# Two expert-choice layers of an eight-layer network: five stages become one, and the expert products move between the search steps

## The reference, cut to what matters

```python
logits = xf @ router_w + router_b          # 2048 x 16
S = softmax(logits, axis=-1)
G, idx = top_k(S.T, k)                     # k = 2048 / 16 = 128, per expert
out = einsum('ekh,hd->ekd', xf[idx], expert_w) + expert_b
y[idx] += G[..., None] * out
```

## Time and profile before

| what | before |
|---|---|
| median of 3 runs | 3193.43 us |
| the profiled execution, its time | 3191.56 us |
| its span, first to last instruction | 3188.7 us |
| PE busy | 89% |
| DVE busy | 53% |
| ACT busy | 26% |
| POOL busy | 31% |
| mean granted TensorE clock | 0.929 of full speed |
| first expert-choice layer, DVE's first to last instruction | 2483.52 to 2594.17 us |
| second one | 3070.68 to 3180.31 us |

### The profile page before, as it was taken

The page is one execution under the profiler, slowest core; times in us unless marked ns, Lnnn a source line. Parts: engine busy times, 40 slices in busy tenths (PEclk is TensorE's granted clock), DMA queues, the critical chain, the costliest instruction groups (busy, mean ns, idle before and its releaser), DMA issues. The chain is left out here.

```text
span 3188.7 us, 46399 instructions
## 1 busy us (share of the span) xinstructions
PE 2822.7 (89%) x15610; PEld 1928.5 (60%) x15610; DVE 1675.7 (53%) x4583; ACT 827.0 (26%) x1344; POOL 974.7 (31%) x1089
## 2 busy tenths in 40 slices
PE   7999999998999999999979999999999538888872
PEld 3444458885556555788757777777777423443451
DVE  5566646666564655466644333333335556555555
ACT  2333344442101011444422222222221002222210
POOL 0000036775444444667721222222221001212200
PEclk8999999999999999999989999999998757887885
DMA  3000020000000000100000000000000000000000
GB/s 137 1 0 0 0 99 1 0 0 1 1 0 0 0 0 0 80 0 0 0 14 14 14 1 14 14 14 1 14 1 1 23 0 1 1 0 0 0 0 26
DMA packets 6281, 37.88 MB, mean 12 GB/s; under 512 B 272, under 2 KB 4368, under 8 KB 4496
## 3 DMA queue, kind: packets, MB, share of 16 engines
q1 hardware_dynamic: 6160, 36.34, 2.9%
HBM read 34.24 MB, written 2.10 MB: 11 GB/s over the span
## 5 line engine op out<-in xcount | busy, mean ns | idle before, releaser
L590 PE MATMUL banks<-back 32*128 32x512 f32 (+3 forms) x1088 | 366.3, 603 | 30.0 <-DVE back L600 20.7
L365 PE MATMUL banks<-moe_parts 128*128 128x512 f32 x1536 | 369.9, 397 | 13.8 <-POOL moe_parts L445 8.9
L817 ACT ACTIVATE back<-banks 128x1024 f32<-128x1024 f32 (+3 forms) x256 | 217.1, 863 | 460.9 <-PE banks L711 460.6
L365 PEld LDWEIGHTS banks<-moe_parts 128*128 128x128 f32 x1536 | 289.1, 192 | 77.2 <-issue 18.9
L1433 PE MATMUL banks<-lin_parts 128*128 128x512 f32 x1152 | 305.9, 411 | 19.3 <-DVE lin_parts L1684 15.5
L1619 DVE TENSOR_TENSOR ffn_pack<-banks,back 128x512 f32<-128x512 f32 x128 | 88.4, 691 | 351.0 <-PE banks L1446 350.9
L711 PE MATMUL banks<-back 32*128 32x512 f32 (+3 forms) x1024 | 242.2, 585 | 20.6 <-DVE back L833 12.5
L1433 PEld LDWEIGHTS banks<-lin_parts 128*128 128x128 f32 x1152 | 212.5, 193 | 67.2 <-issue 21.0
L590 PEld LDWEIGHTS banks<-back 32*128 32x128 f32 x1088 | 135.8, 200 | 185.7 <-DVE back L604 77.7
L1749 POOL TENSOR_TENSOR ffn_pack<-ffn_pack 128x256 f32<-128x256 f32 x112 | 82.9, 741 | 497.2 <-ACT ffn_pack L1582 497.2
L604 DVE TENSOR_REDUCE back<-banks 128x1 f32<-128x512 f32 x272 | 176.3, 686 | 80.2 <-PE banks L590 75.5
(11 more groups left out here) (224 smaller groups left out, 5235.7 us busy)
## 6 DMA issues: line engine op xcount, KB each, us to landing
back<-p_raw SPq DMA_DIRECT2D x8, 1024.0 KB, 4.8
back<-p SPq DMA_DIRECT2D x1, 7696.0 KB, 21.2
ffn_pack<-ffn SPq DMA_DIRECT2D x1, 6144.0 KB, 26.7
back<-p SPq DMA_DIRECT2D x1, 5152.0 KB, 15.0
back<-p SPq DMA_DIRECT2D x2, 1792.0 KB, 8.0
out<-x SPq DMA_DIRECT2D x1, 2048.0 KB, 7.5
x<-x_in SPq DMA_DIRECT2D x1, 1536.0 KB, 12.7
small_pack<-small SPq DMA_DIRECT2D x1, 619.0 KB, 4.9
```

The lines of the kernel that those rows point to most:

```text
L365: mm = nc.tensor.matmul(bank[:], up[:, n % 2, a, which, kd, :], xp[:, b, kd, :], start=((a, b, kd) == (0, 0, 0)), stop=((a, b, kd) == (1, ...
L590: nc.tensor.matmul(bank[:, 0:n], qs[head_rows[j], hg, qi * P:(qi + 1) * P], ks[head_rows[j], hg, 0:n], start=True, stop=True).then_inc(D.f ...
L817: nc.scalar.activation(pt[:, (kt % 2) * 2 + pair, :, q0:T], two[:, :, q0:T], ACT.Exp, scale=0.25).then_inc(A.free.s, 2)
```

## The change

The five blocks become one, without loops.

- Statistics are taken for batches 1 to 3 only (12 tiles). The four instances of the transposed tokens have memory of their own: `c.xt` for batch 0, `xts` for the others. ACT copies each transposed batch out of a pair of PSUM banks in one instruction, where DVE copied two halves.
- The router products are separated from the expert products. PE does all the router products first. The 16 expert products (one for each tile of 128 tokens) follow: two before the transpose of the probabilities, and one behind each of the first 14 counts of the search.
- ACT takes the expert products out of PSUM, two tiles at a time, and POOL adds the bias.
- The search is 15 steps written out. `thr` is updated and `bit` shifted (into a second copy) while PE sums the counts, and one instruction builds the next candidates from `bit`, `thr` and the digit.
- DVE fills `ones`, `thr` and `bit` at the start of the layer; ACT runs one exponential there. A transpose that nothing used and its copy are gone.

```diff
-    D.open(KD + 2 + 2)
     ...
-            with pe.Fori(0, B) as it:
     ...
-                turn_xn(nc, c, pe, it)
+    REST = (B - 1) * NT
     ...
+    xt_of = [c.xt] + [xts[:, b] for b in range(B - 1)]
+    xn_of = [None, c.xn, xn2, c.xn]
+
+    def after_count(u):
+
+        return range(0, 2) if u < 0 else range(u + 2, u + 3) if u + 2 < B * NT else ()
+
     with nc.Block() as block:
         @block.tensor
     ...
+            def turn(b):
+                pe.wait_ge(c.xn_ready.s, c.xn_ready.at(0, b))
+                pe.wait_ge(S.free.s, S.may_fill(0))
+                pair = S.fill("xt", b)
     ...
+            def router(b):
+                if b:
+                    pe.wait_ge(S.free.s, S.released(0, "xt", b))
+                pe.wait_ge(D.free.s, D.may_fill(0))
     ...
+            def product(n):
+                b, i = n // NT, n % NT
+                if i % 2 == 0:
+                    pe.wait_ge(O.free.s, O.may_fill(0))
     ...
+            router(0)
+            for b in range(1, B):
+                turn(b)
+                router(b)
+            for n in after_count(-1):
+                product(n)
+            pe.wait_ge(c.s_ready.s, c.s_ready.at(0, 1))
     ...
+            for u in range(STEPS):
+                pe.wait_ge(c.sum_ready.s, c.sum_ready.at(0, u + 1))
+                pe.wait_ge(D.free.s, D.may_fill(0))
+                bank = D.fill("count", u)
+                nc.tensor.matmul(bank[:, 0:3], same, cnt[:], start=True, stop=True).then_inc(D.full.s, 1)
+                for n in after_count(u):
+                    product(n)
     ...
         @block.scalar
         def _(act):
+            act.wait_ge(c.s_small.s, 16)
+            nc.scalar.activation(warm, c.ident[:, 0:1], ACT.Exp)
+            for b in range(1, B):
+                act.wait_ge(S.full.s, S.may_read(0))
+                pair = S.read("xt", b)
+                nc.scalar.activation(xts[:, b - 1], pair[:], ACT.Identity).then_inc(S.free.s, 1)
     ...
+            for n in range(B * NT // 2):
+                keep_y(n)
 
         @block.vector
     ...
+            moments(nc, c, c.ve, lambda n: c.x[:, 1 + n // NT, n % NT, :], REST)
+            inverse_sqrt(nc, c, c.ve, c.mv[:, 0:REST, 1])
+            norm(1)
+            norm(2)
+            keep_logits(0)
+            dve.wait_ge(S.full.s, S.full.at(0, 1))
+            norm(3)
+            for b in range(1, B):
+                keep_logits(b)
     ...
-            with dve.Fori(0, ROUNDS) as it:
-                c.ve.turn(dve, it)
-                link = c.ve.link
-                for u in range(STEPS):
-
-                    link(nc.vector.tensor_tensor(cand[:], thr.to_broadcast([P, 3]), bit[:], ALU.bitwise_or))
     ...
-                    link(nc.vector.tensor_tensor(add[:], digit[:], bit[:, 0:1], ALU.mult))
-                    nc.vector.tensor_scalar(bit[:], bit[:], 2, None, ALU.logical_shift_right)
-                    link(nc.vector.tensor_tensor(thr[:], thr[:], add[:], ALU.bitwise_or))
     ...
+            for u in range(STEPS):
+                now, later = bit[:, u % 2], bit[:, (u + 1) % 2]
     ...
+                ins.then_inc(c.sum_ready.s, 1)
+                if u:
+                    nc.vector.tensor_tensor(thr[:], thr[:], add[:], ALU.bitwise_or)
+                nc.vector.tensor_scalar(later, now, 2, None, ALU.logical_shift_right)
     ...
+                link(nc.vector.tensor_tensor(add[:], digit[:], now[:, 0:1], ALU.mult))
+                if u + 1 < STEPS:
+                    link(nc.vector.scalar_tensor_tensor(out=cand[:], in0=later, scalar=add[:],
+                                                        in1=thr.to_broadcast([P, 3]), op0=ALU.bitwise_or,
+                                                        op1=ALU.bitwise_or))
     ...
+            dve.wait_ge(c.y_ready.s, c.y_ready.at(0, B * NT // 2))
     ...
+        @block.gpsimd
+        def _(pool):
+            pool.wait_ge(c.s_small.s, 16)
+            for n in range(B * NT // 2):
+                b, h = n // 2, n % 2
+                pool.wait_ge(O.free.s, O.released(0, "y", b, h))
+                ys = y[:, b, 2 * h:2 * h + 2, :]
+                nc.gpsimd.tensor_tensor(ys, ys, eb.unsqueeze(1).to_broadcast([P, 2, DM]), ALU.add)\
+                    .then_inc(c.y_ready.s, 1)
```

More of the change, by code:

```diff
@@ L1865, in _ @@
[L1865 to L1872, removed]
-                for i in range(NT):
[L1874 to L1881, removed]
-                                            bank[:, 0:2 * E6].rearrange("p (a e) -> p a e", a=2),
-                                            rb.unsqueeze(1).to_broadcast([P, 2, E6]), ALU.add)\
-                        .then_inc(D.free.s, 1)
-                for h in range(2):
-                    dve.wait_ge(D.full.s, D.may_read(it))
-                    bank = D.read("out", h)
-                    nc.vector.tensor_tensor(y[:, it, 2 * h:2 * h + 2, :],
-                                            bank[:].rearrange("p (a d) -> p a d", a=2),
-                                            eb.unsqueeze(1).to_broadcast([P, 2, DM]), ALU.add)\
-                        .then_inc(D.free.s, 1)
-                keep_xt(nc, c, dve, it)
@@ L1894, in _ @@
[L1894 to L1904, removed]
-    c.ex_ready.open(1)
-    c.ve.open(4)
-    tiles = lg[:].rearrange("p b i e -> p (b i) e")
-    with nc.Block() as block:
+            def turn(b):
+                pe.wait_ge(c.xn_ready.s, c.xn_ready.at(0, b))
+                pe.wait_ge(S.free.s, S.may_fill(0))
+                pair = S.fill("xt", b)
+                for kd in range(KD):
+                    for i in range(NT):
+                        mm = nc.tensor.transpose(pair[:, kd, i * P:(i + 1) * P],
+                                                 xn_of[b][:, i, kd * P:(kd + 1) * P], c.ident[:])
+                mm.then_inc(S.full.s, 1)
@@ new lines, in _ @@
+            pe.wait_ge(c.sum_ready.s, c.sum_ready.at(0, STEPS + 2))
+            pe.wait_ge(D.free.s, D.may_fill(0))
+            bank = D.fill("taken")
+            nc.tensor.matmul(bank[:, 0:1], same, cnt[:, 0:1], start=True, stop=False)
+            nc.tensor.matmul(bank[:, 0:1], earlier, cum[:, SEG_T - 1:SEG_T], start=False, stop=True)\
+                .then_inc(D.full.s, 1)
+            pe.wait_ge(c.sum_ready.s, c.sum_ready.at(0, STEPS + 3))
+            pe.wait_ge(D.free.s, D.may_fill(0))
@@ L1952, in _ @@
             nc.vector.tensor_copy(ss[:], bank[:, 0:SEG_T]).then_inc(D.free.s, 1)
-            dve.wait_ge(D.full.s, D.may_read(0))
-            bank = D.read("unused")
-            nc.vector.tensor_copy(cnt[:], bank[:, 0:3]).then_inc(D.free.s, 1)
-            nc.vector.memset(ones[:], 1.0)
-            nc.vector.memset(thr[:], 0)
-            for k in range(3):
-                nc.vector.memset(bit[:, k:k + 1], (k + 1) << (BITS - 2))
-    D.close(1)
-    O.take(c.banks[7:8])
-    O.open(STEPS)
@@ L1995, in choice_layer @@
[L1995 to L2024 removed]
+            dve.wait_ge(D.free.s, D.released(0, "turn"))
```

197 lines of the change are left out of this document (92 added, 105 removed).

## The result

The changed kernel takes 3151.72 us in the median of 4 runs (3148.38 to 3154.12), the kernel before 3193.65 (3193.4 to 3199.03): a ratio of 0.9864, with a 95% interval of 0.9847 to 0.9881. That is 41.9 us less; forecast were 48.5, and a time of 3145 in a range of 3126 to 3162.

What follows compares the result with a forecast made beforehand. No engine bounds the layer, but one chain of hand-overs: router part 26.1, softmax 4.6, search 43.0 and selection 12.2 make 85.9 us a layer, saving 48.5 in two. Forecast 3145 us, range 3126 to 3162.

Steps and rivals of the forecast that it cites:

- First normalisation done at 9.2: Layer's start: statistics of 12 tiles, root and first normalisation end 9.2 us after the layer's first DVE instruction.
- softmax: From the softmax's first reduction to the first count: 4.6 us, bounds 4.3 and 5.6, against 5.28 before.
- selection: From the search's last instruction to the layer's end, selection and update: 12.2 us.
- a step without an addition: Search step free of GpSimd's additions: 2.64 us cold, against 2.89 before; 2.45 at full PE clock.
- additions in every second step that hold the digit's product: Search: seven GpSimd additions delay a two-operand DVE instruction, 0.88 us each cold, 0.5 warm.
- rival A: Search and most of router stretch at full PE clock, additions miss DVE's two-operand instructions: 3128 us, chance 0.18.
- C: Search: expert products become the bound, each next count waits behind one, steps of 5.11: 3207 us, chance 0.03.
- D: Search: moved work comes back to within 6 us, steps of 4.2 to 4.8: 3190 us, chance 0.03.
- counts that run on under an addition: Search: DVE's counts are not held by GpSimd's additions; if they were, the two layers take 5 us more.
- the clock of the router stretch: Three batches of transposes and router products: 20.4 us cold, 12.5 warm, taken at the middle, 16.5.
- the hold and the search: The 15 search steps with GpSimd's holds: 45.8 us cold, 40.3 warm, taken at 43.0.
- rival B: PE stays at clock 0.50 throughout and each addition is met in full: 3158 to 3162 us, chance 0.14.

Runs made afterwards that it cites:

- everything together: Changed kernel with batch 0's expert products first, two pairs of PSUM banks for the transposes, and GpSimd's additions timed beside the counts: 3120.12 us.
- the run with two pairs of banks: Changed kernel with a second pair of PSUM banks, each batch's transposes queued ahead of the previous batch's router products: 3131.42 us.

## Why the prediction was right, and by how much it was off

*Right, as forecast.* The saving is that of a chain whose links were taken out, 41.0 us in the two layers for 48.5. First normalisation done at 9.2; softmax 4.24 (4.6); selection 12.12 (12.2); a step without an addition 2.63 (2.64); additions in every second step that hold the digit's product (rival A out); the products hidden behind the counts (C and D out); counts that run on under an addition. No table load of ACT came onto the path.

*Mis-sized: the clock of the router stretch.* The term was three batches between 12.5 warm and 20.4 cold, taken at 16.5. Measured are 19.7, all of it cold, and this is 3.1 of the 3.7 us by which a layer is longer than forecast; two layers make 6.2 of the 7.5 us missing in the two. The step that failed is the inference behind the middle value, which carried the old loop's clock (0.78 at 69% busy) over to a stretch about as busy. It is busier, 83%, and its clock is 0.50. Here a share of busy time didn't carry the clock from one mixture of work to another. What had gone from the loop were the expert products, rows of 16 passes of 256 columns; left were transposes of 128, router passes of 16 and gaps. In the old loop the router products took 1.95 in each of the four turns, at 1.00 (one of them in the earlier trace rows); now they take 3.59. Wider router passes, with the gaps as they were, bring 4.7 to 4.9 us of the part back; gaps filled with passes of 256 columns 4.4 to 4.7. Why the mixture that is left stays at 0.50 remains open.

*Mis-sized: the hold and the search.* The prediction took 43.0 between cold and held (45.8) and warm (40.3). The search was cold (0.53 in the mean), and the hold 0.70 and not 0.88. The digit's product is due 0.24 after the start of an addition of 1.09, so 0.85 of the addition are left. The product ends together with it, as the pair in the earlier trace rows did, so its own 0.16 lie inside them; the prediction added them on top. 15 x 2.63, less 0.2 for a first step at clock 1.00 and a little for the last, and 7 x 0.70, is 44.0.

*Luck.* 43.0 was the middle between a cold search and a warm one, and the search was not in between: it was cold but for its first step, and all seven additions held. That the forecast came within 1.0 us is owed to the smaller hold. What the profile shows is rival B, cold and held, which had a chance of 0.14 and 3158 to 3162. B's terms were each a little too large: 6.8 us for a cold batch that took 6.5, 0.88 for a hold of 0.70. So the forecast's time was nearer than B's time, and B's mechanism nearer than the forecast's.

*Not of the change.* In the profiled pair, 2.7 us are lost ahead of the first layer; the attention between the layers took 476.51 before and 476.52 after.

## What to carry to other kernels

When work is moved off a stretch, look at what is left on PE there: the passes that went may have been the ones under which the clock was high, and the others then cost nearly double (3.59 us for 1.95 here). In a row of narrow passes, widening them from 16 to 128 columns cost almost nothing here (3.62 against 3.59 us for sixteen) and brought the clock up. Where a single result is waited for, as in the search's sums, it cost 0.2 us a step at clock 0.50: alone the wide sums still won 1.5 us a search, with everything together they lost 1.2 to 1.9. Two engines that meet once per step are cheaper to shift against each other than to speed up: a wait that moved six of GpSimd's additions (by 0.85 us for the one shown, which starts 6.90 us behind the addition before and not 6.05) was worth 4.2 us a layer, and shortening the step around them gave back half of its gain as a longer hold.

## What the runs showed of the hardware that was not expected

PE can be busy without a pause and lose its clock: in the run with two pairs of banks it fell from 1.00 to 0.50 at 2505.2, in the middle of passes of 16 columns. A row of transposes went before a rise: in the same run PE had done sixteen of them without a gap, and then only the first few router passes, when the clock rose at 2501.8. In the search of the changed kernel PE is busy for 34.49 of 43.83 us, mostly in passes of 256 columns (2.05 us of its 2.50 in a step), and the clock is 0.50 but for the first step; wide sums brought it up in some of the steps only. Why it stays down in the rest is open.

The attention between the layers, the same instructions in every run, took from 467.7 to 477.9 us in the profiles, and the start of the first layer came between 2483.5 and 2491.5. The stretch of the whole attention, in the changed kernel and in the run with everything together:

```profile
2575.84:3052.36 476.52, 394.82 (x2220) 195.57 (x2220) 259.05 (x1223) 109.11 (x165) 88.11 (x276) 0.82 0.00 1
```

```profile
2563.16:3032.07 468.91, 386.27 (x2220) 191.81 (x2220) 259.10 (x1222) 109.34 (x165) 88.52 (x276) 0.83 0.00 1
```

DVE, ACT and GpSimd do the same work in the same time; PE is busy 8.6 us longer in the slower one, at a lower mean clock. So of the 32.9 us between these two spans, 28.0 are the two layers' and 7.6 the attention's, less 2.6 for a later start. Whether the edit's other timing brings the attention's clock up, or chance does, no run here tells.
